# Pair stage on one core: GpSimd's gathers and scatters spaced by cleared scratch columns instead of by steps

## The chip, the cores and the metric

One Trainium2 chip, one of its cores. The metric is the device time of one execution in microseconds (us). The kernel is written in Bass: each engine (TensorE = PE, VectorE = DVE, ScalarE = ACT, GpSimd = POOL, SyncE = SP) has its own instruction stream, and the streams meet at semaphores. PEld is PE's loading of weights.

## The reference

The input x has 16 batches of 256 tokens with 256 features, 4096 tokens in all. It is normalised once (xn), and the output is x + attention(xn) + experts(xn).

- Attention: xn is normalised again and projected to h (128 features). For every pair (i, j) of a batch, `relu(h_i - h_j + b1)` goes through a 128 to 64 layer with relu and a 64 to 1 layer; that gives a 256 x 256 table of similarities per batch. For each row i the 25 highest entries are found, and attention with 32 heads of width 2 runs over these 25 tokens alone. Then comes an output projection and a residual.
- Experts: a router picks 2 of 8 experts for each token, each expert takes at most 1280 token slots; there are a gated MLP per expert and one shared gated MLP over all tokens.

The pair layers are by far the largest part: 16 x 256 x 256 pairs.

## The kernel before

Tokens are in 32 tiles of 128 (two tiles, "halves", per batch). The program has these stages.

1. **Start**: both layernorms, the router's logits, projections, batch by batch. Keys and values of all tokens are stored to HBM as `kv_rows`, normalised tokens as `xn_rows`.
2. **Pair stage**: 16 batches x 32 steps. In a step, DVE and ACT make 8 rows of first-layer activations (`relu1_row` L1329 on DVE, L1084 on ACT), PE multiplies them (`layer2`, L896), ACT applies the second relu (`relu2`, L1132), and `layer3` (L908) gathers the similarities of the batch in one PSUM bank. `l2_done` counts the steps that PE has done. DVE's instruction order is written out by hand in `pair_batch`: between its rows it puts the work on earlier tiles. `take_sims` (L1445) takes a batch's similarities at step 5 of the next batch; steps 6 to 10 of each half (16 steps) find the 25 best of a tile (L1453, L1459, L1460) and write the gather indices (`topk_rows`, L1465, semaphore `idx_ready`); one half later, at step 12, `weigh` (L1473) multiplies the gathered keys with the queries. `weigh` waits for all 25 gathers of its tile, and DVE's queue is in order: rows of later steps stand behind it. After it come `add_pairs`, `find_max`, `less_max`, and in the half after that `times_values` (L1493) and the folds (L1503).
3. **Experts**: 40 groups of 256 slots through expert weights, then the shared MLP over all tokens and the output. Parts of the last four tiles' attention are done here.

**GpSimd in the pair stage** issues the indirect transfers. First, for `FIRST_PUT` = 9 batches' worth of tile pairs, `scatter_early(i)` scatters 4 x 128 token rows each to the expert slots: 36 transfers (L679), in a row, each batch's four waiting only for the load of those rows. Then, when all of them have landed, come the gathers: 25 per tile (`gather_tile`, L725), each fetching one of the 25 keys and values for 128 rows. Between the two tiles of a batch, `scatter_tile` (L679) does two of the remaining scatters. So a batch has `ROW` = 52 transfers. The code for batches 1 to 13 is a hardware loop on GpSimd; batch 0 stands ahead of it. `gather_tile` waits for `idx_ready`, and for the buffer (two tiles deep) to be free again. Before each of the 52 transfers, save the first of each tile, `pace` waits until PE's step counter `l2_done` has reached a step that grows evenly over 32 steps. Tile 28 (= NT - 4) and later ones are gathered by other waits (`gather_turn`), which the change does not touch. Who waits for these transfers: `weigh` on DVE for the gathers; the loads of expert slots, after the stage, for the scatters. `zeros` and the scratch after it lie in a part of the arena that holds nothing else in this stage.

```
def pace(b, op):
    if op % EVERY == 0:
        wait_alone(pool, "pool", l2_done, b * BSTEPS + (BSTEPS + GATHER_AT + op * BSTEPS // ROW))
```

Of the kernel before, what the change touches and what calls it, by code (L numbers as in the profile page):

```python
# [5 lines left out]
def lsn_attention_moe_block(  # L6
# [33 lines left out]
    HALVES = S // P  # L40
# [22 lines left out]
    BSTEPS = HALVES * STEPS  # L63
# [9 lines left out]
    NCH = NT // CT  # L73
    BEHIND = 3
    XE = 4
    RING = 4
    AHEAD = 2

# [8 lines left out]
    with ctx:  # L87
# [3 lines left out]
        def sem(name):  # L91
            return ctx.enter_context(nc.semaphore(name))
# [28 lines left out]
        def halves(name, n, *dims):  # L121

            pair = []
            for half in ("high", "low"):
                pair.append(nc.alloc_sbuf_tensor_at(f"{name}_{half}", [P, *dims], f32r, offset=arena_at + 4 * taken[0]))
                part(n)
            return pair
# [6 lines left out]
        def part(n, *dims):  # L134
            at = taken[0]
            taken[0] = at + n
            assert taken[0] <= ARENA
            view = arena[:, at:at + n]
            if len(dims) == 1:
                return view.rearrange("p (a b) -> p a b", a=dims[0])  # L140
            if len(dims) == 2:
                return view.rearrange("p (a b c) -> p a b c", a=dims[0], b=dims[1])
            return view
# [34 lines left out]
        taken[0] = rows_base + R1 * STEP_ROWS * S  # L178
        kvs = part(HALVES * 2 * KD, HALVES)
        zeros = part(SLOTS // P * D // NB)  # L180
        assert taken[0] <= attn_base

        taken[0] = attn_base
# [13 lines left out]
        FIRST_PUT = 9  # L197
# [29 lines left out]
        taken[0] = 0  # L227
        xe = [part(2 * D, 2) for _ in range(XE)]
        wug_r, wdn_r, wug, wdn = [], [], [], []
# [23 lines left out]
        xnb = part(CT * D, CT)  # L253
        hTs_r = [halves(f"hTs{i}", 512, 512) for i in range(RING)]
        xT_r.append(halves("xT1", DC * 512, DC, 512))
# [75 lines left out]
        counts_ready = sem("counts_ready")  # L331
        route_done = sem("route_done")
        scattered = sem("scattered")

        r1_dve = sem("r1_dve")
        r1_act = sem("r1_act")
        l2_done = sem("l2_done")
# [10 lines left out]

        xe_loaded = [sem(f"xe_loaded{i}") for i in range(XE)]
        wug_loaded = [sem(f"wug_loaded{i}") for i in range(2)]  # L350
# [55 lines left out]
        GATHER_AT = 9  # L406
# [14 lines left out]
        def wait_alone(eng, name, what, value):  # L421

            eng.wait_ge(what, value)
            eng.sem_inc(passed[name], 1)
# [26 lines left out]
        def slot_rows(m):  # L451
            return slice(0, P) if m < JC else slice(KD, KD + TAIL)

        def ps_heads():
            return ps[0:KD, 3, :]

        def ps_out(n, tiles=1):
            return ps[:, 4 + n:4 + n + tiles, 0:D]
# [5 lines left out]
        def _(sp):  # L464
# [74 lines left out]
            def expert_rows(dram, g):  # L539

                return dram[ds(g // GPE * CAP, CAP), :].rearrange("(p n) d -> p n d", p=P)[:, 2 * (g % GPE):2 * (g % GPE) + 2, :]
# [11 lines left out]
            def load_slots(g):  # L553
                sp.dma_start(xe[g % XE], expert_rows(slot_dram, g)).then_inc(xe_loaded[g % XE], 16)

# [8 lines left out]
            sp.wait_ge(scattered, 16 * 2 * NT)  # L564
            for g in range(XE):
                load_slots(g)
# [17 lines left out]
            for g in range(ALL):  # L584
                if g + XE < ALL:

                    sp.wait_ge(xt_done, g + 1)
                    load_slots(g + XE)
                if g >= BEHIND:
# [45 lines left out]
        def _(pool):  # L635
# [36 lines left out]
            def pace(b, op):  # L672

                if op % EVERY == 0:
                    wait_alone(pool, "pool", l2_done, b * BSTEPS + (BSTEPS + GATHER_AT + op * BSTEPS // ROW))

            def put(rows, slots):

                pool.indirect_dma_start(out=slot_dram, out_offset=bass.IndirectOffsetOnAxis(ap=slots, axis=0), in_=rows, in_offset=None,  # L679
                                        bounds_check=SLOTS - 1, oob_is_err=False).then_inc(scattered, 16)  # L680

            def scatter_early(i):

                wait_alone(pool, "pool", early_staged[i], 16)
                for h in range(HALVES):
                    for k in range(2):
                        n = (i * HALVES + h) * 2 + k
                        put(early_rows[i][:, h, :], slot_put[:, n:n + 1])

            def scatter_tile(b):  # L690

                wait_alone(pool, "pool", staged, b * 32 + 32)
                for k in range(2):
                    pace(b, TOPK + k)
                    put(xstage[:, 0, :], istage[:, k:k + 1])
# [3 lines left out]
            def hold(what, count):  # L699

                if count > held.get(what.name, 0):
                    held[what.name] = count
                    wait_alone(pool, "pool", what, count)

            def gather_turn(t, r):

                if t == NT - 4:
                    return l2_done, NB * BSTEPS - BSTEPS + GATHER_AT + r * (BSTEPS - GATHER_AT) // TOPK
                if t == NT - 1 and r >= IN_GROUPS:
                    return sgu_done, 1 + (r - IN_GROUPS) // 2  # L710
                return gu_done, GATHER_GROUP[t] + r * 5 // 8

            def gather_tile(b, h, first, paced, rows=range(TOPK)):

                t = b * HALVES + h
                wait_alone(pool, "pool", idx_ready, t + 1)
                if not first:

                    wait_alone(pool, "pool", attn_step, (t - 2) * AS + PV_DONE)
                for r in rows:  # L720
                    if r and r < paced:
                        pace(b, h * (ROW - TOPK) + r)
                    if r >= paced and t >= NT - 4:
                        hold(*gather_turn(t, r))
                    pool.indirect_dma_start(  # L725
                        out=kvg[:, h, r, :], out_offset=None, in_=kv_dram,
                        in_offset=bass.IndirectOffsetOnAxis(ap=gidx[:, h, r:r + 1], axis=0)).then_inc(gathered[h], 16)
# [32 lines left out]

            GATHER_GROUP = {NT - 3: 0, NT - 2: 16, NT - 1: 32}
            IN_GROUPS = 13
            EVERY = 1
            ROW = HALVES * TOPK + 2
            for i in range(FIRST_PUT):
                scatter_early(i)

            wait_alone(pool, "pool", scattered, 16 * 2 * HALVES * FIRST_PUT)
            gather_tile(0, 0, True, TOPK)
            scatter_tile(0)  # L770
            gather_tile(0, 1, True, TOPK)
            with pool.Fori(1, NB - 2) as b:
                gather_tile(b, 0, False, TOPK)
                scatter_tile(b)
                gather_tile(b, 1, False, TOPK)
# [42 lines left out]
        def _(pe):  # L818
# [113 lines left out]
            def products(to, weights, moving, first, last_one):  # L932

                for i, (a, b) in enumerate(((0, 0), (0, 1), (1, 0))):
                    mm = nc.tensor.matmul(to, weights[a], moving[b], start=(first and i == 0), stop=(last_one and i == 2))  # L935
                return mm
# [87 lines left out]
            def shared_down(q):  # L1024
# [11 lines left out]
                for n in range(CT):  # L1036

                    last = products(ps_out(n)[:, 0, :], [h[:, n * P:(n + 1) * P] for h in hTs_r[q % RING]],
                                    [w[:, m, :] for w in swdn_r], m == 0, m == JC)
# [18 lines left out]
        def _(act):  # L1058
# [187 lines left out]
            def slot_high(q):  # L1246
                rows = slot_rows(q % SM)
                act.wait_ge(smul_done, q + 1)
                nc.scalar.activation(hTs_r[q % RING][0][rows, :], sgs[q % 2][rows], ACT.Copy).then_inc(shigh_done, 1)

            def heads_high(c):
                act.wait_ge(aoT_done, c + 1)
                nc.scalar.activation(hTs_r[(c * SM + JC) % RING][0][0:KD, :], ps_heads(), ACT.Copy).then_inc(aoT_high, 1)

# [19 lines left out]
        def _(dve):  # L1274
# [406 lines left out]
            def slot_low(q):  # L1681
                rows = slot_rows(q % SM)
                high, low = hTs_r[q % RING]
                dve.wait_ge(shigh_done, q + 1)
                nc.vector.tensor_tensor(low[rows, :], sgs[q % 2][rows], high[rows, :].bitcast(f32), ALU.subtract).then_inc(slow_done, 1)  # L1685

            def heads_low(c):
                high, low = hTs_r[(c * SM + JC) % RING]
                dve.wait_ge(aoT_high, c + 1)
                nc.vector.tensor_tensor(low[0:KD, :], ps_heads(), high[0:KD, :].bitcast(f32), ALU.subtract).then_inc(aoT_low, 1)  # L1690
# [87 lines left out]
```

## Time and profile before

| | us |
|---|---|
| median of 3 runs | 1815.98 (1804.49 to 1820.84) |
| the profiled execution | 1798.93 |
| its span, first to last instruction | 1797.2 |

The profiled execution is 17 us under the median. Busy shares of its span: PE 93%, DVE 83%, ACT 80%, GpSimd 62%. The costliest groups of the page are the gathers on GpSimd (L725, x800, 897.8 us busy, 1122 ns each), the second-layer matmuls (L896, x4096, 979.0 us), the second relu on ACT (L1132, x512, 638.2 us), and the first-layer rows on DVE (L1329, x2368) and ACT (L1084, x1620). Busy PE time is not PE at its peak, since matmuls are pipelined and their ends are modelled. Idle time of an engine that is not the bottleneck costs nothing; "remote" as a releaser is a wait whose end the profile cannot put down to an engine of this core.

### The profile page before, as it was taken

What the parts mean: (1) busy time and instruction counts of PE and PEld (TensorE: products, weight loads), DVE (VectorE), ACT (ScalarE), POOL (GpSimd) and SP (SyncE); (2) the same over time, 40 slices, a digit from 0 to 9 for tenths busy, and PEclk for the clock granted to TensorE, in tenths of its full rate; (3) what the DMA queues carried; (4) which work ended last, traced back from release to release, by engine and by line L of the source; (5) the groups of instructions that cost most, each with busy time, mean ns of one, the idle gap of its engine ahead of it and who ended that gap; (6) DMA issues with size and microseconds to landing.
All of it is one profiled execution on the core that took longest, in us unless ns stands there. A gap on an engine that the chain in (4) does not pass through costs nothing.

```text
span 1797.2 us, 30702 instructions
## 1 busy us (share of the span) xinstructions
PE 1662.6 (93%) x9092; PEld 721.4 (40%) x9092; DVE 1499.8 (83%) x4205; ACT 1443.6 (80%) x2787; POOL 1114.1 (62%) x1009
## 2 busy tenths in 40 slices
PE   7995999899999999989999999899999999998998
PEld 6731222222222222222222222222222499997887
DVE  6891578889889989979898988899899688866888
ACT  5693899889899989979998989899999877843342
POOL 3207067767776677777676767777676644355556
PEclk9997899999999999989999999999999999999999
DMA  5623011111111111111111111111131166532333
GB/s 190 249 85 113 7 41 49 48 44 49 40 50 45 48 42 50 46 40 49 43 46 42 51 44 47 42 49 49 45 94 39 51 198 205 180 122 74 117 118 105
DMA packets 80074, 136.87 MB, mean 76 GB/s; under 512 B 22337, under 2 KB 46529, under 8 KB 79937
## 3 DMA queue, kind: packets, MB, share of 16 engines
q0 software_dynamic: 31744, 69.27, 13.8%
q1 hardware_dynamic: 48192, 65.91, 11.1%
q8 instruction: 70, 1.15, 0.3%
q14 instruction: 68, 0.55, 0.1%
HBM read 95.24 MB, written 39.85 MB: 75 GB/s over the span
## 4 chain that ended last, share of the span: by engine, by line
PE 39%; ACT 36%; issue 8%; DVE 5%; another core or an unknown queue 4%; DMA 1%; POOL 1%; SPq 0%; POOLq 0%; ACTq 0%; DVEq 0%
ACT arena L1084 22%; PE ps L896 20%; PE ps L935 14%; ACT arena L1132 13%; PE ps L908 5%; DVE arena L1329 2%; PE ps L952 1%; ACT arena L1136 1%; DVE top L1453 0%; DMA arena<-xn_rows 0%; DVE hTs_low L1685 0%; DVE idx L1460 0%; DVE arena L1459 0%; POOL arena L806 0%
## 5 line engine op out<-in xcount | busy, mean ns | idle before, releaser
L725 POOL DMA_INDIRECT arena<-kv_rows,gidx x800 | 897.8, 1122 | 475.3 <-issue 221.0
L896 PE MATMUL ps<-arena,w2t 128*64 128x512 f32 x4096 | 979.0, 603 | 96.4 <-ACT arena L1132 47.3
L1132 ACT ACTIVATE arena<-ps,b 128x1024 f32<-128x1024 f32 x512 | 638.2, 1251 | 143.4 <-remote 95.6
L896 PEld LDWEIGHTS ps<-arena,w2t 128*64 128x64 f32 x4096 | 280.7, 137 | 785.2 <-issue 675.4
L1329 DVE TENSOR_SCALAR arena<-arena 128x256 f32<-128x256 f32 x1184 | 368.6, 368 | 106.7 <-remote 64.7
L1329 DVE TENSOR_SCALAR arena<-h_now 128x256 f32<-128x256 f32 x1184 | 371.7, 370 | 59.4 <-PE ps L896 39.3
L1084 ACT ACTIVATE arena<-ps,h_now 128x256 f32<-128x256 f32 x864 | 381.7, 634 | 0.0
L1084 ACT ACTIVATE arena<-ps,arena 128x256 f32<-128x256 f32 x756 | 332.8, 617 | 0.0
L908 PE MATMUL ps<-arena,w3win 128*32 128x512 f32 x2048 | 278.7, 608 | 3.9 <-issue 3.9
L908 PEld LDWEIGHTS ps<-arena,w3win 128*32 128x32 f32 x2048 | 41.2, 108 | 215.7 <-issue 161.0
L1503 DVE TENSOR_TENSOR arena<-arena 128x1152 f32<-128x1152 f32 (+4 forms) x160 | 100.3, 627 | 0.4
L806 POOL DMA_INDIRECT arena<-slot_outputs,slot_get x64 | 70.3, 1099 | 29.1 <-issue 16.2
L1244 ACT ACTIVATE off_diag<-ps 128x512 f32<-128x512 f32 (+1 forms) x24 | 14.3, 597 | 75.7 <-PE ps L935 44.5
L679 POOL DMA_INDIRECT slot_inputs<-arena,slot_put x36 | 38.8, 1077 | 52.5 <-issue 52.5
L935 PE MATMUL ps<-xTe_high,wug_high 128*112 128x256 f32 (+1 forms) x240 | 70.5, 294 | 0.0
L935 PE MATMUL ps<-xT_high,swug_low 128*128 128x512 f32 x176 | 69.2, 393 | 1.2 <-issue 1.2
L935 PE MATMUL ps<-xT_high,swug_high 128*128 128x512 f32 x176 | 70.0, 398 | 0.2 <-DVE off_diag L1679 0.2
L935 PE MATMUL ps<-xT_low,swug_high 128*128 128x512 f32 x176 | 69.3, 394 | 0.0
L935 PE MATMUL ps<-xTe_low,wug_high 128*112 128x256 f32 (+1 forms) x240 | 67.5, 281 | 0.0
L935 PE MATMUL ps<-xTe_high,wug_low 128*112 128x256 f32 (+1 forms) x240 | 67.3, 280 | 0.0
L660 POOL TENSOR_TENSOR arena<-arena 128x2 f32<-128x2 f32 x32 | 24.0, 765 | 61.2 <-DVE arena L1293 61.2
L1473 DVE TENSOR_TENSOR arena<-arena,qao 128x1600 f32<-128x1600 f32 x32 | 58.3, 1821 | 3.4 <-DMA arena<-kv_rows,gidx 1.6
(157 smaller groups left out, 2092.0 us busy)
## 6 DMA issues: line engine op xcount, KB each, us to landing
arena<-kv_rows,gidx POOLq DMA_INDIRECT x800
slot_inputs<-arena SPq DMA_DIRECT2D x16, 640.0 KB, 3.8
arena<-slot_inputs SPq DMA_DIRECT2D x40, 256.0 KB
slot_outputs<-arena SPq DMA_DIRECT2D x40, 256.0 KB
arena<-in_L_attn_x_dram SPq DMA_DIRECT2D x16, 256.0 KB, 2.9
xn_rows<-arena SPq DMA_DIRECT2D x16, 256.0 KB, 3.8
arena<-in_L_attn_x_dram SPq DMA_DIRECT2D x8, 512.0 KB
arena<-xn_rows SPq DMA_DIRECT2D x8, 512.0 KB
```

The costliest lines, as they stand in the source:

```text
L660: nc.gpsimd.tensor_tensor(rstd[:, r, :], veps[:, r, :], neg_half, ALU.pow).then_inc(rstd_ready[r], 1)
L679: pool.indirect_dma_start(out=slot_dram, out_offset=bass.IndirectOffsetOnAxis(ap=slots, axis=0), in_=rows, in_offset=None, bounds_check=SL ...
L725: pool.indirect_dma_start(out=kvg[:, h, r, :], out_offset=None, in_=kv_dram, in_offset=bass.IndirectOffsetOnAxis(ap=gidx[:, h, r:r + 1], a ...
L806: pool.indirect_dma_start(out=ys[c % 2][:, n, k, :], out_offset=None, in_=yslot_dram, in_offset=bass.IndirectOffsetOnAxis(ap=slot_get[:, c ...
L896: last = nc.tensor.matmul(ps_l2(n)[v * G2:(v + 1) * G2, u, :], w2t[:, :], r1[:, n % R1, 4 * u + 2 * v:4 * u + 2 * v + 2, :], start=True, s ...
L908: last = nc.tensor.matmul(ps[32 * c:32 * c + 32, 6, :], w3win[:, at:at + 32], r2[:, (2 * q + c // 2) % R2, 512 * (c % 2):512 * (c % 2) + 512],
L935: mm = nc.tensor.matmul(to, weights[a], moving[b], start=(first and i == 0), stop=(last_one and i == 2))
L1084: last = nc.scalar.activation(r1[:, n % R1, k, :], hneg_now[i] if first else ps_hneg[i], ACT.Relu, bias=hb_now[i][:, at:at + 1])
L1132: nc.scalar.activation(r2[:, n % R2, :].rearrange("p (u n) -> p u n", u=2), ps_l2(n), ACT.Relu, bias=b2[:, 0:1]).then_inc(r2_done, 1)
L1329: row = nc.vector.tensor_scalar(r1[:, (b * BSTEPS + s) % R1, k, :], hneg_now[i], hb_now[i][:, at:at + 1], 0.0, ALU.add, ALU.max)
L1473: nc.vector.tensor_tensor(prod, kvg[:, h, :, 0:KD], qao[:, ds(t, 1), :].to_broadcast([P, TOPK, KD]), ALU.mult)\
L1503: nc.vector.tensor_tensor(pve[:, 0:n, :], pve[:, 0:n, :], pve[:, rows - n:rows, :], ALU.add).then_inc(attn_step, 1)
```

## The change

Three things in GpSimd's stream. `pace` no longer waits for PE's steps: it calls `rest`, which clears 1200 columns of a scratch area (`idle_cols`, 128 partitions, f32) and waits until that has completed. `EVERY` becomes 3, so `pace` does so ahead of each transfer of a batch whose number is a multiple of 3: 3, 6, ..., 51, that is 17 rests for 52 transfers. The first gather of a batch's second tile, which had no `pace` before, has one now (number 27). In `scatter_early` a rest follows each second scatter: 18 rests for 36 scatters. The waits for indices, for free buffers and for loaded rows stay. Tiles 28 and later are as before.

```diff
--- before.py
+++ after.py
@@ -73,6 +73,7 @@
     NCH = NT // CT
     BEHIND = 3
     XE = 4
+    IDLE = 1200
     RING = 4
     AHEAD = 2
 
@@ -178,6 +179,7 @@
         taken[0] = rows_base + R1 * STEP_ROWS * S
         kvs = part(HALVES * 2 * KD, HALVES)
         zeros = part(SLOTS // P * D // NB)
+        idle_cols = part(IDLE)
         assert taken[0] <= attn_base
 
         taken[0] = attn_base
@@ -331,6 +333,7 @@
         counts_ready = sem("counts_ready")
         route_done = sem("route_done")
         scattered = sem("scattered")
+        rested = sem("rested")
 
         r1_dve = sem("r1_dve")
         r1_act = sem("r1_act")
@@ -672,7 +675,12 @@
             def pace(b, op):
 
                 if op % EVERY == 0:
-                    wait_alone(pool, "pool", l2_done, b * BSTEPS + (BSTEPS + GATHER_AT + op * BSTEPS // ROW))
+                    rest(b * RESTS + (FIRST_PUT * HALVES + op // EVERY))
+
+            def rest(count):
+
+                nc.gpsimd.memset(idle_cols, 0.0).then_inc(rested, 1)
+                wait_alone(pool, "pool", rested, count)
 
             def put(rows, slots):
 
@@ -686,6 +694,7 @@
                     for k in range(2):
                         n = (i * HALVES + h) * 2 + k
                         put(early_rows[i][:, h, :], slot_put[:, n:n + 1])
+                    rest(i * HALVES + h + 1)
 
             def scatter_tile(b):
 
@@ -718,7 +727,7 @@
 
                     wait_alone(pool, "pool", attn_step, (t - 2) * AS + PV_DONE)
                 for r in rows:
-                    if r and r < paced:
+                    if r + h and r < paced:
                         pace(b, h * (ROW - TOPK) + r)
                     if r >= paced and t >= NT - 4:
                         hold(*gather_turn(t, r))
@@ -760,8 +769,9 @@
 
             GATHER_GROUP = {NT - 3: 0, NT - 2: 16, NT - 1: 32}
             IN_GROUPS = 13
-            EVERY = 1
+            EVERY = 3
             ROW = HALVES * TOPK + 2
+            RESTS = (ROW - 1) // EVERY
             for i in range(FIRST_PUT):
                 scatter_early(i)
```

## Rows read from the trace of the kernel before

**Rows 1.** Busy time by engine in two stretches (columns named in the first line).

```profile
core 0: us, PE busy (x) PEld busy (x) DVE busy (x) ACT busy (x) POOL busy (x), PEclk, DMA share, GB/s
224.30:1369.00 1144.70, 1069.60 (x5402) 282.09 (x5400) 1015.23 (x2962) 1037.05 (x2007) 820.10 (x728) 0.99 0.17 48
150.00:200.00 50.00, 27.00 (x80) 5.85 (x79) 9.73 (x35) 17.53 (x34) 23.80 (x25) 0.69 0.19 67
```

**Rows 2.** Groups on POOL, 224.3 to 1368.9 us: busy, mean ns | idle before.

```profile
L725 POOL DMA_INDIRECT arena<-kv_rows,gidx x700 | 789.0, 1127 | 357.1 <-issue 179.8 <-PE ps L896 81.8 <-remote 50.9
L679 POOL DMA_INDIRECT slot_inputs<-xstage,istage x28 | 31.1, 1111 | 10.6 <-issue 8.0 <-PE ps L896 2.3 <-DVE qao L1511 0.3
```

**Rows 3.** POOL in order of time: start us, us, instruction [idle before <-releaser].

```profile
224.25 3.66 POOL L725 DMA_INDIRECT arena<-kv_rows,gidx  x1 [43.12 <-DVE gidx L1465]
254.21 0.98 POOL L725 DMA_INDIRECT arena<-kv_rows,gidx  x1 [1.73 <-PE ps L896]
...
275.35 0.95 POOL L725 DMA_INDIRECT arena<-kv_rows,gidx  x1 [0.30 <-issue]
...
796.37 1.20 POOL L725 DMA_INDIRECT arena<-kv_rows,gidx  x1 [3.51 <-remote]
...
1367.99 0.95 POOL L725 DMA_INDIRECT arena<-kv_rows,gidx  x1 [0.30 <-issue]
```

**Rows 4.** DVE in order of time: two of the products with gathered keys.

```profile
715.32 1.83 DVE L1473 TENSOR_TENSOR arena<-arena,qao 128x1600 f32<-128x1600 f32 x1 [0.30 <-DMA arena<-kv_rows,gidx]
...
1370.56 1.83 DVE L1473 TENSOR_TENSOR arena<-arena,qao 128x1600 f32<-128x1600 f32 x1 [0.15 <-issue]
```

**Rows 5.** POOL in order of time, start of the program: memory cleared.

```profile
0.91 1.16 POOL L637 MEMSET arena<- 128x1280 f32 x1
...
2.49 0.52 POOL L642 MEMSET off_diag<- 128x512 f32 x1
```

**Rows 6.** POOL in order of time, three changes between kinds of instruction.

```profile
1420.87 1.70 POOL L735 TENSOR_TENSOR wug_low<-arena,wug_high 128x704 fp32r<-128x704 f32 x1 [0.19 <-POOL wug_high L733]
...
1601.70 1.23 POOL L725 DMA_INDIRECT arena<-kv_rows,gidx  x1 [0.15 <-issue]
...
1623.71 1.68 POOL L806 DMA_INDIRECT arena<-slot_outputs,slot_get  x1 [0.30 <-issue]
1625.41 2.36 POOL L756 TENSOR_TENSOR arena<-arena 128x1024 f32<-128x1024 f32 x1
```

**Rows 7.** POOL in order of time: two gathers longer than the others.

```profile
731.79 1.43 POOL L725 DMA_INDIRECT arena<-kv_rows,gidx  x1 [0.30 <-issue]
733.52 1.89 POOL L725 DMA_INDIRECT arena<-kv_rows,gidx  x1 [0.30 <-issue]
```

**Rows 8.** DVE in order of time, the same moments.

```profile
730.51 1.88 DVE L1493 TENSOR_TENSOR arena<-arena 128x1600 f32<-128x1600 f32 x1
...
733.24 1.34 DVE L1503 TENSOR_TENSOR arena<-arena 128x1152 f32<-128x1152 f32 x1
```

**Rows 9.** DVE in order of time: its first-layer rows without and with gathers beside them.

```profile
213.03 1.92 DVE L1329 TENSOR_SCALAR arena<-h_now 128x256 f32<-128x256 f32 x7
...
275.86 4.58 DVE L1329 TENSOR_SCALAR arena<-arena 128x256 f32<-128x256 f32 x14
```

**Rows 10.** DVE in order of time: one shape twice, in the last stage.

```profile
1596.12 0.69 DVE L1685 TENSOR_TENSOR hTs_low<-off_diag,hTs_high 128x512 fp32r<-128x512 f32 x1
...
1625.08 3.25 DVE L1685 TENSOR_TENSOR hTs_low<-off_diag,hTs_high 128x512 fp32r<-128x512 f32 x1
```

**Rows 11.** POOL in order of time: first and last of the 36 early scatters.

```profile
131.66 4.75 POOL L679 DMA_INDIRECT slot_inputs<-arena,slot_put  x1 [41.77 <-issue]
...
180.15 0.97 POOL L679 DMA_INDIRECT slot_inputs<-arena,slot_put  x1 [0.31 <-issue]
```

**Rows 12.** PE in order of time, beside the early scatters.

```profile
144.52 3.65 PE L896 MATMUL ps<-arena,w2t 128*64 128x512 f32 x16
148.10 1.07 PE L908 MATMUL ps<-arena,w3win 128*32 128x512 f32 x8
...
157.21 1.77 PE L896 MATMUL ps<-arena,w2t 128*64 128x512 f32 x2 [0.42 <-issue]
173.91 3.68 PE L896 MATMUL ps<-arena,w2t 128*64 128x512 f32 x8 [14.94 <-issue]
...
187.79 4.47 PE L896 MATMUL ps<-arena,w2t 128*64 128x512 f32 x16
```

## The prediction

> **What bounds the kernel now.** I read first the busy time by stretch, then GpSimd's groups, then GpSimd and DVE in order of time around the wait of interest. The stretch is that of the changed code: from the first gather (224.25 us) to the end of the last gather of tile 27 (1367.99 + 0.95 = 1368.9 us) [rows 3]. These 1144.7 us hold 14 batches of 52 transfers, so a batch takes 81.8 us. PE is busy 1070 us of them, ACT 1037, DVE 1015 [rows 1]: three balanced engines, none at the limit for all of it. PE's own pace, 16 second-layer and 8 third-layer records in 148.10 + 1.07 - 144.52 = 4.65 us for two steps [rows 12], would be about 74 us a batch; what is over it are waits among the three engines.
>
> GpSimd looks harmless with 820 us busy for 728 transfers [rows 1, 2]. It isn't. In a run of transfers each has 0.30 us ahead of it that nothing of the kernel explains [rows 3], 728 x 0.30 = 218 us. The idle time of the groups is 357.1 + 10.6 us, of which 43.1 lie before the first gather [rows 2, 3], so 324.6; less 218, **106 us are true waiting**, 7.6 us per batch: for PE's steps, as at 254.21, and for indices, as at 796.37 [rows 3]. So GpSimd needs 820 + 218 = 1038 us of the 1144.6, 74 us of each 82 us batch. That the transfers come just in time is seen at their reader: the product at 715.32 waited 0.30 us for its gathers, and the one at 1370.56 began 1.6 us after its tile's last gather was issued [rows 3, 4]. DVE's later rows stand behind that product, so a late gather stops DVE, then PE and ACT.
>
> **The change, part by part.**
>
> *Removed: the step waits.* They hold no work; without them GpSimd may begin a tile when its indices are there. That frees at most the 106 us, as room and not as time saved, since the stage goes by the other three engines.
>
> *Added: 17 rests in each of 14 batches, 238.* 1280 columns take 1.16 us and 512 take 0.52 [rows 5], 0.84 ns a column, so 1200 take 1.09. A compute instruction began right behind a transfer (1623.71 + 1.68 against 1625.41: 0.02 us), one that waited for its own engine's result began 0.19 behind it, and a transfer behind a computation 0.15 behind it [rows 6]. The transfer behind a rest must wait for the semaphore and then be issued, which is not shown; I take 0.30, the gap of transfers behind each other, as the nearest. A rest replaces one such gap, so it costs 0.02 + 1.09 + 0.30 - 0.30 = **1.11 us**. Lower bound, with 0.15 behind: 0.96. Upper bound, if the next transfer also takes 1.23 instead of 0.95, as one did behind a computation [rows 3, 6]: 1.39. For 238: 228, **264**, 331 us. Nothing covers it, because each rest is waited for.
>
> *Unchanged: collisions.* The transfers' excess over 0.95 us, 820 - 728 x 0.95 = 128 us, comes where DVE combines two long operands: the gathers of 1.43 and 1.89 us lie on such operations [rows 7, 8]. DVE does as many of them as before; I keep the 128 and, as a bound, halve it, since some of them may meet a rest instead.
>
> *Sum for the stretch:* 1038 + 264 = 1302 us, 93 us a batch. That is more than the 82 that the other engines need with all their waits. **GpSimd becomes the bound**: DVE waits at each product, and the stretch grows by 1302 - 1145 = 157 us. Two tiles of buffer hold no reserve against it: the lag grows until it reaches the product and stays there.
>
> *The early scatters* run from 131.66 to 181.1 [rows 11], and GpSimd then waits 43 us for the first indices [rows 3]. 18 rests add 18 x 1.11 = 20 us, to 201, inside that wait. But in this stretch something else is to be had: PE did nothing from 159.0 to 173.9 and reached full pace only at 187.8, two steps in 38.6 us, where they take 4.6 [rows 12]; the granted clock's mean from 150 to 200 us is 0.69 [rows 1]. Some 33 us are lost, while the scatters were issued without a pause. I can't name the mechanism, but in the gathers, where GpSimd pauses, the stretch as a whole shows no such loss (PE busy 1070 of 1145). With a pause after every second scatter I take it as mostly gone. The first gather then begins when the scatters end and have landed, about 205 instead of 224: **-19 us**. Bound on one side 224.2 - 33 = 191 for the indices, which the scatters' end makes 202: -22. On the other the stall stays and lasts as long as the scatters, 20 us more: +20.
>
> *After tile 27* nothing changes: its product, then 20 steps to the stage's end, and the experts.
>
> Sum: 1798.9 + 157 - 19 = **1937 us**, on the profiled execution's base. The median of before lies 17 us above that base, so against the median it is +6.7%. I add nothing for the 17 us: an execution bounded by GpSimd's fixed sequence should hang less on how the others meet.
>
> **A rule weighed against the trace.** DVE's first-layer rows take 1.92 us for 7 without gathers (0.274 each) and 4.58 for 14 beside them (0.327) [rows 9]; 0.74 us more over some 3.6 gathers, so a transfer holds DVE up by 0.2 us. And one DVE operation of 0.69 us took 3.25 while GpSimd added two tiles [rows 6, 10]. The Trainium skill (SBUF — State Buffer, "SBUF: two separate sides") says that DVE and GpSimd share a port pair as an exclusive lock for a whole instruction: against DVE's two-port modes, and against its operations with two SBUF inputs where GpSimd reads too. By that rule a rest, which only writes, would stop DVE's rows, which is the first rival, and leave the two-operand operations alone, which would favour the third; the trace agrees for transfers and two-operand additions and shows no clearing beside DVE rows.
>
> **The rivals.**
>
> 1. *DVE becomes the bound, or both.* Place: the first-layer rows beside each rest. Price: up to 1.09 us x 238 = 259 us on DVE, 1015 + 259 = 1274 busy; if its 129 us of other waits stay too, 1404 us for the stretch, +259 - 19, so **2039 us**. It decides over GpSimd's chain when a rest costs DVE more than (1302 - 1145) / 238 = 0.66 us and none of DVE's waits are absorbed. For: rows 9 and 10. Against: the waits are for PE and ACT, which have over 200 us of room then, so most would be absorbed and the stretch would stay near 1300. Chance 0.14.
> 2. *The early stall stays*, with rests and all: 1937 + 39 = **1976 us**. For: the cause is unknown, and scatters in pairs are still scatters. Chance 0.15.
> 3. *The other side: faster.* If the collisions vanish (DVE's long operations meet rests, which don't mind them) and a rest costs its lower bound, GpSimd needs 728 x 1.25 + 228 = 1138 us, no more than the stretch has now, and the 33 us of the early stall are saved: **1766 us**. It decides when rests and collisions together stay under 106 + 128 = 234 us, against 392 in my sum. Against: GpSimd would have to be clear of DVE's long operations, with nothing that arranges it. Chance 0.05.
> 4. *In between:* collisions halve and a rest costs 0.96: 1038 - 64 + 228 = 1202, +57 - 22, **1834 us**, at the edge of what can be told. Chance 0.06.
>
> That the clearing isn't done is excluded by its semaphore, on which GpSimd waits.
>
> **How the numbers follow.** My forecast has 0.60, with 1937 us; the cost of a rest at 1.25 instead of 1.11 would make it 1970, at 1.0 with somewhat fewer collisions 1890. The range for 8 in 10 leaves out rivals 3 and 4 (0.11) and the top of rival 1: 1860 to 2010. One per cent, 18 us, is what a measurement of this kernel can tell from no change. Faster by over 1%: rival 3, 0.05. Within 1%: most of rival 4, 0.06. Slower: 0.89.
>
> **What would show it.** The profile after should have 256 clearings of about 1.1 us; 728 transfers and 238 clearings between the first gather and the end of tile 27's gathers, in about 1300 us with GpSimd idle little beyond the gaps; nearly every product on DVE (L1473) waiting several us for its gathers; PE, ACT and DVE shares of that stretch down to about 80%; between 150 and 190 us no stop of PE. Wrong would be: GpSimd waiting for indices in most tiles (then another engine bounds), DVE rows of over 1 us beside a clearing with DVE idle little (rival 1), transfers of 0.95 throughout (rival 3).

## The result and the profile after

The changed kernel takes 2043.2 us (median of 4 runs, 2039.07 to 2051.04), the kernel before 1812.95 (4 runs, 1804.49 to 1820.84): a ratio of **1.131, 95% interval 1.126 to 1.135**. The forecast was 1937 us, with a range of 1860 to 2010. The profiled execution took 2045.24 us. In kernel.py of after the names sit ten lines further on: the gathers are L734, the scatters L687, the clearing L682, DVE's first-layer rows L1339, the product L1483.

The first gather starts at 214.8 us (224.25 before [rows 3]), tile 27's last gather ends at 1615.6, and 429.6 us follow, as before (1798.9 - 1368.9 = 430). So all of it lies in the stretch: 1400.8 us against 1144.7. Busy time by stretch (us, PE busy (count), PEld, DVE, ACT, POOL, PEclk, DMA share, GB/s), to be set beside [rows 1]:

```profile
214.80:1615.60 1400.80, 1094.66 (x5324) 264.74 (x5320) 1248.12 (x2925) 1046.48 (x1990) 1041.66 (x966) 0.95 0.14 39
150.00:200.00 50.00, 46.08 (x242) 11.75 (x240) 42.97 (x105) 47.33 (x93) 35.77 (x35) 1.00 0.18 62
```

PE and ACT have about the work they had and 256 us more room. GpSimd has 1042 us, 222 more, and DVE 1248, 233 more. The second line is the early stall's: PE is busy for 46 of 50 us where it was for 27. The groups of GpSimd in the stretch, as in [rows 2]:

```profile
L734 POOL DMA_INDIRECT arena<-kv_rows,gidx x700 | 744.9, 1064 | 350.7 <-POOL arena L682 196.5 <-issue 153.0 <-DMA slot_inputs<-arena,slot_put 1.3
L682 POOL MEMSET arena<- 128x1200 f32 x238 | 265.6, 1116 | 0.1
L687 POOL DMA_INDIRECT slot_inputs<-xstage,istage x28 | 32.0, 1143 | 9.6 <-issue 9.6
```

No wait for indices or buffers is left; 744.9 + 265.6 + 32.0 us of work and 360.4 us of idle make up the stretch to 2 us. 196.5 us of the idle time stand behind the clearings. GpSimd in order of time shows each of them:

```profile
212.36 1.11 POOL L682 MEMSET arena<- 128x1200 f32 x1
214.79 3.68 POOL L734 DMA_INDIRECT arena<-kv_rows,gidx  x1 [1.32 <-DMA slot_inputs<-arena,slot_put]
...
803.87 1.11 POOL L682 MEMSET arena<- 128x1200 f32 x1
805.81 0.96 POOL L734 DMA_INDIRECT arena<-kv_rows,gidx  x1 [0.83 <-POOL arena L682]
807.08 0.95 POOL L734 DMA_INDIRECT arena<-kv_rows,gidx  x1 [0.30 <-issue]
808.34 0.95 POOL L734 DMA_INDIRECT arena<-kv_rows,gidx  x1 [0.30 <-issue]
809.29 1.12 POOL L682 MEMSET arena<- 128x1200 f32 x1
811.23 0.96 POOL L734 DMA_INDIRECT arena<-kv_rows,gidx  x1 [0.83 <-POOL arena L682]
```

From one clearing to the next are 5.42 us, three transfers' worth of which is 3.77: **a rest costs 1.65 us, 0.83 of it after the clearing has ended**. DVE, by groups and then in order of time:

```profile
L1339 DVE TENSOR_SCALAR arena<-arena 128x256 f32<-128x256 f32 x1036 | 456.9, 496 | 0.0
L1483 DVE TENSOR_TENSOR arena<-arena,qao 128x1600 f32<-128x1600 f32 x27 | 49.5, 1835 | 146.9 <-DMA arena<-kv_rows,gidx 146.9
```

```profile
803.43 1.96 DVE L1339 TENSOR_SCALAR arena<-h_now 128x256 f32<-128x256 f32 x2
806.32 0.86 DVE L1339 TENSOR_SCALAR arena<-h_now 128x256 f32<-128x256 f32 x3
813.78 1.83 DVE L1483 TENSOR_TENSOR arena<-arena,qao 128x1600 f32<-128x1600 f32 x1 [6.60 <-DMA arena<-kv_rows,gidx]
```

Three rows take 0.86 us, so two take 0.57; two beside the clearing at 803.87 take 1.96, about 1.4 more. Over the program the 2368 rows of DVE average 484 ns and 369 before, and hold DVE for 270 us more: 1.05 for each of the 256 clearings, an average in which some clearings meet no row. Still DVE waits at these 27 products, 5.4 us each on average (28.3 at the first). PE passes the wait on, as its costliest group shows, and the page's chain of waits runs along GpSimd:

```profile
L906 PE MATMUL ps<-arena,w2t 128*64 128x512 f32 x3548 | 878.9, 627 | 304.6 <-DVE arena L1339 298.7 <-issue 3.8
```

```profile
POOL 50%; issue 23%; PE 17%; DVE 2%; ACT 1%; DMA 1%; POOLq 1%; another core or an unknown queue 1%; SPq 0%; DVEq 0%; ACTq 0%
```

### The profile page after: what moved, and what is told of

Read it like the earlier page. It is cut to its first block, busy times and chain, and to the rows that moved or that the text cites. A ratio compares the mean times of both kernels' runs of the same rounds, so it can differ in the third digit from the quotient of the medians.

```text
span 2043.5 us, 30319 instructions
## 1 busy us (share of the span) xinstructions
PE 1692.3 (83%) x9092; PEld 706.5 (35%) x9092; DVE 1767.5 (86%) x4205; ACT 1462.8 (72%) x2787; POOL 1357.4 (66%) x1265
## 4 chain that ended last, share of the span: by engine, by line
POOL 50%; issue 23%; PE 17%; DVE 2%; ACT 1%; DMA 1%; POOLq 1%; another core or an unknown queue 1%; SPq 0%; DVEq 0%; ACTq 0%
POOL arena L734 33%; POOL arena L682 14%; PE ps L945 13%; POOL slot_inputs L687 3%; PE ps L906 2%; PE ps L962 1%; PE ps L918 1%; DVE hTs_low L1695 0%; POOLq L427 0%; DMA arena<-slot_inputs 0%; DVE xTe_low L1604 0%; ACT hTe_high L1219 0%; DVE arena L1713 0%; DVE arena L1483 0%
## 5 line engine op out<-in xcount | busy, mean ns | idle before, releaser
L906 PE MATMUL ps<-arena,w2t 128*64 128x512 f32 x4096 | 1006.6, 624 | 316.0 <-DVE arena L1339 308.1
L734 POOL DMA_INDIRECT arena<-kv_rows,gidx x800 | 854.4, 1068 | 467.9 <-issue 196.5
L1142 ACT ACTIVATE arena<-ps,b 128x1024 f32<-128x1024 f32 x512 | 588.5, 1150 | 364.9 <-PE ps L906 308.9
L906 PEld LDWEIGHTS ps<-arena,w2t 128*64 128x64 f32 x4096 | 266.5, 141 | 1051.1 <-DVE arena L1339 613.1
L1339 DVE TENSOR_SCALAR arena<-arena 128x256 f32<-128x256 f32 x1184 | 505.2, 484 | 5.3 <-PE ps L906 3.1
L1339 DVE TENSOR_SCALAR arena<-h_now 128x256 f32<-128x256 f32 x1184 | 504.7, 483 | 3.4 <-PE ps L906 3.4
L1094 ACT ACTIVATE arena<-ps,h_now 128x256 f32<-128x256 f32 x864 | 355.1, 534 | 0.0
L1094 ACT ACTIVATE arena<-ps,arena 128x256 f32<-128x256 f32 x756 | 305.7, 513 | 0.0
L682 POOL MEMSET arena<- 128x1200 f32 x256 | 285.6, 1116 | 0.2
L1483 DVE TENSOR_TENSOR arena<-arena,qao 128x1600 f32<-128x1600 f32 x32 | 58.7, 1833 | 154.4 <-DMA arena<-kv_rows,gidx 154.3
L1513 DVE TENSOR_TENSOR arena<-arena 128x1152 f32<-128x1152 f32 (+4 forms) x160 | 105.5, 659 | 0.4
L687 POOL DMA_INDIRECT slot_inputs<-arena,slot_put x36 | 39.7, 1102 | 63.6 <-issue 48.4
```

The lines of the kernel that those rows point to most:

```text
L682: nc.gpsimd.memset(idle_cols, 0.0).then_inc(rested, 1)
L734: pool.indirect_dma_start(out=kvg[:, h, r, :], out_offset=None, in_=kv_dram, in_offset=bass.IndirectOffsetOnAxis(ap=gidx[:, h, r:r + 1], a ...
L906: last = nc.tensor.matmul(ps_l2(n)[v * G2:(v + 1) * G2, u, :], w2t[:, :], r1[:, n % R1, 4 * u + 2 * v:4 * u + 2 * v + 2, :], start=True, s ...
L1094: last = nc.scalar.activation(r1[:, n % R1, k, :], hneg_now[i] if first else ps_hneg[i], ACT.Relu, bias=hb_now[i][:, at:at + 1])
L1142: nc.scalar.activation(r2[:, n % R2, :].rearrange("p (u n) -> p u n", u=2), ps_l2(n), ACT.Relu, bias=b2[:, 0:1]).then_inc(r2_done, 1)
L1339: row = nc.vector.tensor_scalar(r1[:, (b * BSTEPS + s) % R1, k, :], hneg_now[i], hb_now[i][:, at:at + 1], 0.0, ALU.add, ALU.max)
```

## The experiments

The kernel before was timed beside each group, on another chip each time, and it differs by chip: 1846.95, 1653.47, 1798.81 and 1794.25 us for the four groups. Ratios are to it on the same chip, with 95% intervals. "The stretch" is again from the first gather to the end of tile 27's.

### First group: what a rest costs, and who pays (before 1846.95 us, 12 runs)

**Wait ahead.** The clearing stays; GpSimd waits for the *previous* one, ahead of it, and for nothing behind it.

```diff
 def rest(count):
+    if count is not None:
+        wait_alone(pool, "pool", rested, count - 1)
     nc.gpsimd.memset(idle_cols, 0.0).then_inc(rested, 1)
-    wait_alone(pool, "pool", rested, count)
...
-                    rest(i * HALVES + h + 1)
+                    rest(i * HALVES + h + 1 if i + h else None)
```

> The changed kernel, but each clearing is not waited for behind it; instead the next clearing waits for it. The columns cleared and their number (256) stay. Theory G (GpSimd's own sequence bounds the stretch, and what I mis-sized is the 0.83 us between a clearing's end and the next transfer): that gap falls to about 0.15, a rest to about 0.97 us net, GpSimd's need for the stretch from 1401 to about 1240 us. Theory V (each clearing holds DVE's rows for its 1.1 us, and that sets the time): no change, 2043 us, since DVE is held as before. DVE's busy time of 1248 us in the stretch stays in both, so under G the stretch can't go under about 1250 and the time comes to 1885 to 1940 us, with DVE now hardly waiting for gathers.

1965.65 us, ratio 1.065 (1.060 to 1.071). By stretch, groups of DVE, and GpSimd in order of time:

```profile
202.40:1526.70 1324.30, 1066.95 (x5332) 255.67 (x5330) 1319.55 (x2923) 1044.27 (x1981) 1080.88 (x966) 1.00 0.15 41
```

```profile
L1340 DVE TENSOR_SCALAR arena<-arena 128x256 f32<-128x256 f32 x1036 | 479.7, 520 | 0.0
L1484 DVE TENSOR_TENSOR arena<-arena,qao 128x1600 f32<-128x1600 f32 x27 | 48.9, 1811 | 4.6 <-DMA arena<-kv_rows,gidx 4.4
```

```profile
604.54 1.12 POOL L684 MEMSET arena<- 128x1200 f32 x1
605.83 1.08 POOL L735 DMA_INDIRECT arena<-kv_rows,gidx  x1 [0.16 <-POOL arena L684]
```

With the wait gone from in front of the transfer, the gap is 0.16 us and not 0.83. The stretch is 77 us shorter, and now DVE is the bound: busy 1319.6 of 1324.3 us, 4.6 us of waiting at 27 products. The time is above the 1885 to 1940 us that I expected, because DVE's load did not stay at 1248 us. Part of that can be counted in the traces: 224 of the 238 clearings fall on a row of DVE here and 201 in the changed kernel, where 19 fell into time in which DVE was idle. The rest of the 72 us is not explained.

**Short clears.** Four clearings of 16 columns, each waited for, take the place of the long one: a rest without a long hold on DVE (`SHORT` = 4).

```diff
-    nc.gpsimd.memset(idle_cols, 0.0).then_inc(rested, 1)
-    wait_alone(pool, "pool", rested, count)
+    for k in range(SHORT):
+        nc.gpsimd.memset(idle_cols[:, 0:16], 0.0).then_inc(rested, 1)
+        wait_alone(pool, "pool", rested, (count - 1) * SHORT + (k + 1))
```

> The changed kernel, but a rest is four clearings of 16 columns, each waited for, instead of one of 1200. Theory G: a rest lasts about 4 x 0.11 + 3 x 0.2 + 0.83 = 1.9 us of GpSimd's time as before (1.94), so the time stays within some 30 us of 2043. Theory V: DVE is held for 0.4 us or less per rest instead of 1.1, so the time falls by up to 238 x 0.7 = 165 us, to about 1880. In both DVE's row mean falls from 484 ns towards 370.

2039.99 us, ratio 1.107 (1.100 to 1.113).

```profile
212.20:1594.10 1381.90, 1078.12 (x5324) 283.58 (x5320) 971.48 (x2919) 1027.17 (x1989) 918.37 (x1680) 0.88 0.15 39
```

```profile
L1485 DVE TENSOR_TENSOR arena<-arena,qao 128x1600 f32<-128x1600 f32 x27 | 49.6, 1837 | 382.1 <-DMA arena<-kv_rows,gidx 382.1
```

DVE's load falls from 1248 to 971 us, and the stretch stays within 19 us of the changed kernel's: what DVE no longer does it waits, 382 us at 27 products. GpSimd bounds the changed kernel. The clock does not: it was granted at 0.88 of full speed here and at 0.95 in the changed kernel, and the stretch with the lower clock is the shorter one.

**16 columns.** `IDLE = 16` in the changed kernel: the wait alone, with next to no clearing.

> The changed kernel with 16 columns per clearing instead of 1200. A rest falls from 1.94 to about 0.94 us (0.64 net of the gap that it replaces). Theory G: GpSimd needs 1401 - 238 = 1163 us for the stretch, against 1145 of the kernel before, and the early stop of PE stays away: about 1805 us, near the kernel before. Theory V gives the same within 20 us; what this run tells is whether anything but the length of the rests makes the change slow: then it stays above 1850.

1824.23 us, ratio 0.989 (0.982 to 0.995), 19 us above the 1805 expected.

```profile
201.60:1390.20 1188.60, 1065.13 (x5380) 276.79 (x5376) 985.16 (x2942) 1034.87 (x2003) 829.72 (x966) 0.95 0.17 46
```

GpSimd is still full: 829.7 us busy, 238 gaps of 0.83 and 490 of 0.30 us come to 1174 of 1188.6 us. So the length of the rests is what made the change slow.

**Early only.** The kernel before with its step waits, and only the 18 early rests of 1200 columns added (the diff is against the kernel before, without the lines that define `rest`).

```diff
                         put(early_rows[i][:, h, :], slot_put[:, n:n + 1])
+                    rest(i * HALVES + h + 1)
```

> The kernel before with one part of the change alone: the rests (1200 columns, waited for) behind each second early scatter; the gathers wait for PE's steps as before. If the scatters without a pause are what stops PE for some 33 us, PE runs through, the first gather begins at about 215 instead of 224 us (the scatters' own end is then what it waits for), and the time falls by about 9 us or a little more. If the stop has another cause it stays, and the time rises by 0 to 20 us.

1828.14 us, ratio 0.990 (0.986 to 0.994).

```profile
215.40:1397.10 1181.70, 1082.90 (x5290) 282.25 (x5288) 989.72 (x2921) 1018.11 (x1967) 856.72 (x728) 0.97 0.17 46
150.00:200.00 50.00, 46.21 (x243) 12.03 (x240) 42.66 (x106) 47.53 (x94) 35.47 (x36) 1.00 0.18 61
```

The early stop is gone. But PE stops later, in 11 places of the stretch, first 18 us into the gathers. So the stops don't belong to the scatters alone.

### Second group: what the pause is for (before 1653.47 us, 23 runs)

**Before again**, profiled on this chip.

> The kernel before, unchanged, for a profile on this chip to hold the others against. Executions of it range from 1804 to 1870 us over two chips. If the stops of PE vary from one execution to the next, the stretch of 14 batches is longer here than 1145 us by as much as the time is above 1799, and waits that end from no engine (95 us on ACT's second relu in the first profile) grow with it.

1657.54 us. Stretches, and the chain of waits:

```profile
191.20:1234.30 1043.10, 1033.18 (x5392) 274.18 (x5392) 1003.75 (x2957) 1028.83 (x2008) 819.09 (x728) 1.00 0.20 52
150.00:200.00 50.00, 49.02 (x258) 13.23 (x256) 33.74 (x116) 50.00 (x100) 32.27 (x31) 1.00 0.22 75
```

```profile
PE 83%; ACT 5%; DVE 2%; DMA 2%; issue 1%; POOL 1%; SPq 0%; POOLq 0%; DVEq 0%; ACTq 0%
```

The same program has no stop of PE on this chip, and PE is busy all through. The stretch is 102 us shorter than that of [rows 1] (1144.7 - 1043.1), so most of what I read there as waits among the three engines was of this other kind. It is spread thin: in the stretch of [rows 1], 122 matmuls started 0.6 to 2.2 us after the one before, 144 us in all; here 11 did, 10 us in all.

**Free run.** No rest in the batches and no step wait; early rests of 16 columns.

```diff
-    IDLE = 1200
+    IDLE = 16
 def pace(b, op):
-    if op % EVERY == 0:
-        rest(b * RESTS + (FIRST_PUT * HALVES + op // EVERY))
+    return
```

> The changed kernel with 16 columns per early clearing and no rests at all in the 14 batches: the gathers wait for neither steps nor clearings. GpSimd then needs about 1040 us for the stretch. Theory P (transfers issued without a pause stop PE, as the early scatters did): runs of 25 to 27 transfers stop PE in each half batch, and the time is at or above the kernel before in spite of the early gain: 1.00 to 1.03 of it. Theory W (the pauses in the batches don't matter, only room on GpSimd does): the stretch falls to what DVE, ACT and PE need, the time to 0.96 to 0.98 of before.

1660.22 us, ratio 1.002 (0.998 to 1.007); the stretch is 1040.3 us. Here the step waits are worth nothing. Neither theory foresaw that: I expected the time to rise with stops or to fall by 2 to 4%.

**Paced, early 16.** The kernel before and 18 early rests of 16 columns.

> The kernel before with early rests alone, of 16 columns instead of 1200. The early scatters end about 18 us earlier than with 1200 columns (near 199 us against 213), so the first gather begins near 201. If the pause of 0.8 us behind a clearing is enough to keep PE going, the time falls to 0.98 to 0.985 of before (0.990 with 1200 columns); if PE needs the longer pause, the stop comes back and it is 0.99 to 1.00.

1656.95 us, ratio 1.002 (0.999 to 1.005).

**Every 6, 16 columns.** `EVERY = 6` and `IDLE = 16`, eight rests a batch.

> The changed kernel with 16 columns per clearing and a rest ahead of every sixth transfer instead of every third: 112 rests of about 0.65 us net in the stretch. GpSimd needs about 1038 - 30 + 73 = 1080 to 1110 us, under the 1145 to 1190 of the others, so DVE should wait little for gathers. If pauses every sixth transfer keep PE going, 0.96 to 0.98 of before; if six transfers in a row are enough to stop it, 0.99 or more. With every third it was 0.989, GpSimd being the bound.

1712.61 us, ratio 1.035 (1.029 to 1.041), above both values expected; the stretch is 1098.4 us. 112 rests of 16 columns lengthen a stretch in which GpSimd was already full: 819 + 728 x 0.30 = 1037 of 1043 us.

### Third group: the same kernels where PE stops (before 1798.81 us, 13 runs)

**After again.**

> The changed kernel, unchanged, timed beside the kernel before on whatever chip this is. Theory C (the kernel before is 1650 us on a chip where PE never stops and 1810 to 1850 where it does, while the changed kernel is bounded by GpSimd's own sequence on either): 2035 to 2050 us here too, whatever the kernel before takes, so a ratio of 1.10 to 1.13 where before is slow and about 1.23 where it takes 1650. If instead the whole chip is quicker, the changed kernel falls in the same proportion, to about 1865.

2046.15 us, ratio 1.138 (1.129 to 1.146), the stretch 1402.7 us: to 2 us that of the first trace.

**Free run again** (the kernel of the second group).

> The kernel without any rest or step wait in the batches (early rests of 16 columns). Where the kernel before takes 1650 us: 1.00 of it again. Where it takes over 1800: theory P (transfers without a pause stop PE on such a chip; in two traces PE's stops came after 10 to 26 transfers in a row) has more stops than before, 1.00 to 1.03; theory W (the stops don't depend on transfers) 0.97 to 0.99.

2049.84 us (2019.73 to 2094.57), ratio **1.130 (1.117 to 1.143)**, where the other chip had 1.002 and I had expected 1.03 at most. The trace is of the longest of its executions, so its shape counts and not its last per cent. Stretch, waits (total, count, mean), PE and GpSimd in order of time:

```profile
200.40:1643.70 1443.30, 1176.49 (x5258) 297.92 (x5256) 965.53 (x2878) 1007.49 (x1950) 787.88 (x728) 0.89 0.14 38
```

```profile
DVE arena L1338 <- remote: 364.9, 43, 20.7
ACT arena L1141 <- remote: 356.2, 43, 20.6
POOL arena L733 <- DVE arena L1512: 426.1, 26, 22.2
```

```profile
487.12 1.72 PE L917 MATMUL ps<-arena,w3win 128*32 128x512 f32 x4
489.34 0.59 PE L917 MATMUL ps<-arena,w3win 128*32 128x512 f32 x1 [0.51 <-issue]
490.74 0.59 PE L917 MATMUL ps<-arena,w3win 128*32 128x512 f32 x1 [0.81 <-issue]
492.15 1.01 PE L917 MATMUL ps<-arena,w3win 128*32 128x512 f32 x1 [0.82 <-issue]
494.24 1.01 PE L917 MATMUL ps<-arena,w3win 128*32 128x512 f32 x1 [1.07 <-issue]
```

```profile
462.21 1.95 POOL L733 DMA_INDIRECT arena<-kv_rows,gidx  x1 [17.72 <-DVE arena L1512]
...
494.80 0.95 POOL L733 DMA_INDIRECT arena<-kv_rows,gidx  x1 [0.30 <-issue]
```

PE thins out to one matmul per 1.4 or 2.1 us and halts, while GpSimd issues 25 transfers in a row; there are some 23 such places, most of them 13 to 26 transfers into a run. GpSimd itself waits 426 us, so it is no bound here.

**Every 6 again.**

> Rests of 16 columns ahead of every sixth transfer. Bounded by GpSimd on either kind of chip, 1700 to 1720 us: 1.035 where the kernel before takes 1650, and where it takes over 1800 about 0.94, if six transfers in a row don't stop PE; if they do, it is 0.98 or more.

1855.63 us, ratio 1.019 (1.009 to 1.029). About ten places with stops, after runs of 0 to 8 transfers. (The trace is of an execution of 1874.20 us.)

**16 columns again.**

> Rests of 16 columns ahead of every third transfer. Bounded by GpSimd: 1815 to 1825 us on any chip, so 1.10 of the kernel before where that takes 1650 us, and 0.98 to 0.99 where it takes over 1800.

1809.76 us, ratio 1.007 (1.002 to 1.011), where 0.98 to 0.99 was expected. In the trace, of the shortest execution (1791.66 us), the stretch is 1166.3 us, without a stop; DVE waits 162 us at its products.

### Fourth group: the 0.83 us, and a version worth having (before 1794.25 us, 23 runs)

**Second clear.** A clearing of 16 columns is waited for; a second one, not waited for, stands between that wait and the transfer.

```diff
-    nc.gpsimd.memset(idle_cols, 0.0).then_inc(rested, 1)
-    wait_alone(pool, "pool", rested, count)
+    nc.gpsimd.memset(idle_cols[:, 0:16], 0.0).then_inc(rested, 1)
+    wait_alone(pool, "pool", rested, (count - 1) * 2 + 1)
+    nc.gpsimd.memset(idle_cols[:, 16:32], 0.0).then_inc(rested, 1)
```

> As the changed kernel, but a rest clears 16 columns, waits for that, and clears 16 other columns without a wait; every third transfer as before. If the 0.83 us belongs to a transfer issued right behind a wait on GpSimd's own result, it falls to about 0.16 here, and the space between two transfers at a rest is 0.12 + 0.11 + 0.12 + 0.16 = 0.5 us instead of 0.95; if it belongs to the wait, it stays 0.83 and comes between the clearings. In the first case GpSimd needs about 1166 - 238 x 0.44 = 1061 us for the stretch; where PE doesn't stop, the time is about 1.00 of before on a chip with 1650 us and 0.95 on one with 1800. If 0.5 us is too short a pause for such a chip, PE stops and it is over 1.00 there.

1804.63 us, ratio 1.006 (1.003 to 1.009).

```profile
618.88 0.15 POOL L682 MEMSET arena<- 128x16 f32 x1
619.18 0.11 POOL L684 MEMSET arena<- 128x16 f32 x1 [0.15 <-issue]
619.88 0.98 POOL L735 DMA_INDIRECT arena<-kv_rows,gidx  x1 [0.59 <-issue]
```

The second clearing starts 0.15 us behind the waited one. The transfer starts 0.15 + 0.11 + 0.59 = 0.85 us behind it, as if the second were not there. That is neither of the two outcomes that I had named. The wait itself costs 0.15 us, as the second clearing shows. The rest goes with the transfer: behind a wait it starts 0.83 to 0.85 us after the awaited clearing's end whether or not an instruction stands between, and where the wait ended a clearing of 1.12 us earlier (wait ahead), 0.16 us suffice. I read it as work on the transfer that begins only when the wait ahead of it is over; no view shows that work itself. A rest costs as much as with one clearing of 16 columns, and so the time didn't fall to the 0.95 expected.

**Every 4, 16 columns.** `EVERY = 4`, `IDLE = 16`.

> Rests of 16 columns ahead of every fourth transfer, 12 per batch. GpSimd needs 728 x 1.255 + 80 to 100 + 168 x 0.65 = 1105 to 1125 us: about 1735 us on a chip without stops (1.05 of 1650). On a chip with stops: as every third (no stop in its trace) 0.96 to 0.97 of 1800, as every sixth (11 stops, 1.02) 1.00 or more.

1800.29 us, ratio 1.003 (0.999 to 1.006). I had expected this if PE stops, and 0.96 to 0.97 if it doesn't. The trace is of the shortest execution (1771.01 us): the stretch is 1145.3 us, with two places of short gaps of PE and no long stop, and DVE waits 120 us at the products.

**Paced, early 16, again** (as in the second group).

> The kernel before with early rests of 16 columns alone. On a chip without stops 1.00 again. On one with stops the early loss of some 30 us is saved if PE keeps going there, and the first gather begins near 196 to 201 us instead of 224: 0.98 to 0.99 of before.

1763.52 us (1761.59 to 1781.62), ratio **0.986 (0.981 to 0.990)**: faster than both kernels, as expected, and no slower on the chip without stops. Only the early stop is gone, as the second line shows: 121 matmuls of the stretch still start 0.6 to 2.2 us after the one before.

```profile
196.20:1328.60 1132.40, 1056.72 (x5376) 279.18 (x5368) 1010.26 (x2949) 1029.39 (x1996) 807.90 (x728) 1.00 0.18 48
150.00:200.00 50.00, 49.02 (x256) 13.02 (x252) 33.84 (x115) 50.00 (x101) 30.73 (x42) 1.00 0.21 74
```

## Why the prediction was wrong, and what of it held

1937 us was 5.2% low, and the time lies above the range. The mechanism and its place were right; **the step that failed is the price of a rest: 1.65 us where I had 1.11 and 1.39 as the upper bound, since the transfer behind a rest, for which I took 0.30 us, started 0.83 us after it**.

- *GpSimd becomes the bound, DVE waits at each product.* Shown: GpSimd has no other wait than gaps, DVE waits 147 us, and taking 277 us off DVE (short clears) moves the stretch by 19 only, while taking 0.67 us off each rest (wait ahead) moves it by 77.
- *238 x 1.11 = 264 us.* Measured 238 x 1.65 = 393. The clearing took 1.116 us (1.09), hardly off. The gap behind it was 0.83 and not 0.30: 126 us more. The 0.30 came from [rows 3], where transfers follow one another, and the 0.15 of the lower bound from [rows 6], where one follows a computation with nothing awaited in between; the upper bound kept the 0.30. Neither follows a wait that has just ended, so the row nearest in kind of instruction was not nearest in kind of event. A row of that kind existed: the first gather [rows 3], at 224.25, began 0.88 us after DVE had written its indices (the row below, of the kernel before). With it a rest would have been 0.02 + 1.09 + 0.88 - 0.30 = 1.69, the stretch 1440 and the time 2075: 1.6% high.

```profile
223.14 0.23 DVE L1465 TENSOR_SCALAR gidx<-idx,batch_row 128x32 uint32<-128x32 uint32 x1
```

- *Collisions kept at 128 us.* Transfers were 776.9 us busy, 82 over 728 x 0.955, so 43 us less than before. They fell, but didn't vanish (rival 3). The sum of the stretch: 1302 + 126 + 6 for the clearings - 43 + 10 for other gaps (what is left over) = 1401, and 1400.8 was measured.
- *The early stall.* It is gone as predicted (rival 2 falls), but the scatters with their rests end at 212.4, since each of the 18 rests costs 1.65 or more too, and the first gather waits for their landing: 214.8 and not 205, a gain of 9.5 us where I had 19.
- *"They hold no work"*, of the step waits. As work true; as a cause false, and for a kernel that removes them without rests it would have been an error of 13%: free run is 1.002 on one chip and 1.130 on another. The stop that I read as the early scatters' own comes among the gathers too. In the changed kernel, no run is longer than four (the last transfer of a batch and the first three of the next), and no stop is in its trace, so this error did not move the number.
- *Rival 1* (2039 us) hits the measured number and is not the mechanism. Its first half is real: the clearings hold DVE's rows, 270 us in all against the 259 I gave it, and that its sum meets 2043 is luck. With GpSimd out of the way (wait ahead) DVE's bound shows: 1320 us of work in 1324. That is 77 us under GpSimd's 1401, and my argument that DVE's other waits would be absorbed held.

The Trainium skill (SBUF — State Buffer, "SBUF: two separate sides") has DVE in a two-port mode and GpSimd exclude each other at a shared port pair for a whole instruction, and a DVE operation with two SBUF inputs only where GpSimd's instruction reads. The traces agree with both halves, though no run shows in which mode the rows are. DVE's rows wait out nearly all of each clearing that they meet. The products with gathered keys, which have two inputs, don't, and run side by side with a clearing:

```profile
763.47 1.82 DVE L1483 TENSOR_TENSOR arena<-arena,qao 128x1600 f32<-128x1600 f32 x1 [1.59 <-DMA arena<-kv_rows,gidx]
...
764.37 1.13 POOL L682 MEMSET arena<- 128x1200 f32 x1
```

11 of the 27 products of the stretch had a clearing beside them and took 1.85 us on average, the other 16 took 1.83; no clearing took more than 1.14. What the transfers met I haven't sorted: 43 us of collisions went and 82 stayed.

Two views at once would have kept me nearer. GpSimd's busy share of 62% hid that it was full: with 0.30 us ahead of each transfer, 1037 of the 1043 us that the other engines need where nothing stops them. And the median of the kernel before hides a loss that depends on the chip: the changed kernel, bounded by a fixed sequence, took 2043 and 2046 us in its two sets of runs, while before took 1653 to 1847 on its chips. The 13% is therefore measured against a stage that already lost about 100 us. The changed kernel wasn't run on the chip where before takes 1653; if it takes the same 2045 there, the ratio would be 1.24, which is an estimate.

**Left open:** what stops PE. Its matmuls come at multiples of about 0.7 us and then halt for up to 15 us, only on some chips, and with transfers issued in long runs (free run, early scatters); but Every 6 again had stops after 0 to 8 transfers, so no length of run decides it. The granted clock doesn't start the stop, as it falls afterwards: in the trace of before it was 1.00 from 150 to 153 us, when the matmuls had already thinned out, and 0.50 (1.2 of 2.4 GHz) from 165 to 186. A wait of GpSimd without any clearing wasn't tried.

## What to carry to other kernels

Price a wait that an engine puts on itself by the instruction behind it: here a DMA issue restarted 0.83 us after the wait, five times the semaphore's own 0.15, and 238 of them cost 200 us. Before loading an engine that shows 62% busy, add the fixed gaps ahead of its instructions; if that fills the stretch, each microsecond added is a microsecond of time. Put a pause only where the burst is: 18 rests of 16 columns behind the early scatters gave 1.4% where PE stops and cost nothing where it doesn't, while rests of 1200 columns spread over all transfers cost 13%, and rests of 16 columns there gave 0.989 and 1.007 of before.

## What the runs showed of the hardware

- An indirect transfer starts 0.30 us behind another, 0.16 behind a clearing that isn't waited for, and 0.83 behind one that is (0.90 to 1.00 among the early scatters), or 0.85 behind it with another instruction between them. A clearing behind a waited clearing starts after 0.15.
- A clearing of 1200 columns (1.12 us) delays DVE's rows by 1.05 us on average, by about 1.4 where it meets one, and DVE's products with two inputs hardly (1.85 us beside one, 1.83 without); one of 16 columns takes 0.11 to 0.16 us, and the rows stay at 0.36 us.
- One program took 1653, 1794, 1799 and 1847 us on four chips. In the two profiled executions (stretches of 1043 and 1145 us) the difference goes with PE's matmuls coming at wide intervals, 11 against 122 of them, at a granted clock of 1.00 and 0.99.
- Without pauses between the transfers, the same kernel was 13% slower than before on one chip and equal to it on another.
